# Half of a projection down, moved from the second scan stage to the second ranking stage of a one-core kernel

## The reference, cut to what matters

```python
x = x + tanh(g_xattn) * mamba(ctx_1024, gate=layernorm(x))     # 4 batches, 1024 steps, 1024 channels, 16 states
h = layernorm(x)
scores = h @ w_router;  idx = sort(top_k(scores, 128))         # 128 rows of each batch
sel = h[b, idx]                                                # 4 x 128 rows
x1  = sel + attention(rms_norm(sel)) @ wo                      # causal over the 512 rows
h2  = rms_norm(x1)
mlp = (silu(h2 @ w_gate) * (h2 @ w_up)) @ w_down               # w_down: 4096 x 1024
out[b, idx] = sigmoid(score) * (x1 + mlp) + (1 - sigmoid(score)) * sel
x = x + tanh(g_ffn) * out
```

## Time and profile before

| what | us |
|---|---|
| median of 3 runs | 3016.49 |
| lowest and highest | 3014.51, 3021.93 |
| the profiled execution's own time | 3018.8 |
| its span, first to last instruction | 3017.1 |

### The profile page before, as it was taken

How to read it: one execution, slowest core, us unless ns; L and a number is a source line. 1 busy time by engine, 2 the same in 40 slices (tenths; PEclk the granted TensorE clock), 3 DMA queues, 4 the chain that set the end, 5 groups by cost and what they waited for, 6 DMA issues and landing times. The chain is left out here.

```text
span 3017.1 us, 30047 instructions
## 1 busy us (share of the span) xinstructions
PE 2392.6 (79%) x10552; PEld 1599.2 (53%) x10552; DVE 2110.9 (70%) x2626; ACT 1338.0 (44%) x2470; POOL 1683.2 (56%) x600
## 2 busy tenths in 40 slices
PE   7857777778777547986888888888883299999998
PEld 3334444444444326653767666654552186668863
DVE  4569999999999674432999999999997633310000
ACT  3457755566655342242665555665552212410000
POOL 1169999999999401003998898999993100000000
PEclk9969999989999758998999999999997599999999
DMA  7722252342522396745236335336333543144543
GB/s 259 253 90 75 67 158 77 113 139 63 164 66 60 115 374 208 287 134 189 84 105 197 99 104 186 109 98 216 98 108 133 204 170 98 50 144 151 152 153 104
DMA packets 224869, 426.70 MB, mean 141 GB/s; under 512 B 17488, under 2 KB 101712, under 8 KB 221904
## 3 DMA queue, kind: packets, MB, share of 16 engines
q1 hardware_dynamic: 211216, 368.68, 38.3%
q10 hardware_dynamic: 12160, 51.39, 4.3%
q0 software_dynamic: 1344, 4.72, 0.4%
HBM read 340.84 MB, written 83.89 MB: 141 GB/s over the span
## 5 line engine op out<-in xcount | busy, mean ns | idle before, releaser
L600 POOL TENSOR_TENSOR s_x<-s_du,k_bB 128x2048 f32<-128x2048 f32 x256 | 1156.3, 4533 | 80.8 <-PE s_py L663 52.0
L896 ACT ACTIVATE s_pA<-s_delta,k_negA 128x512 f32<-128x512 f32 x1024 | 664.1, 680 | 382.7 <-DVE s_x L947 373.9
L663 PE MATMUL s_py<-k_ident,s_x 128*128 128x128 f32 x4096 | 582.8, 289 | 260.6 <-DVE s_x L947 253.2
L663 PEld LDWEIGHTS s_py<-k_ident,s_x 128*128 128x128 f32 x4096 | 506.8, 150 | 489.3 <-DVE s_x L947 347.2
L962 DVE TENSOR_TENSOR_SCAN s_pA<-s_pA,s_x 128x512 f32<-128x512 f32 x384 | 452.2, 1214 | 40.9 <-POOL s_x L600 38.3
L947 DVE TENSOR_TENSOR s_x<-s_pA,k_bC 128x1024 f32<-128x1024 f32 x384 | 464.2, 1209 | 19.1 <-DMA k_bC<-scratch_xd 19.0
L962 DVE TENSOR_TENSOR_SCAN s_pA<-s_pA,s_carry,s_x 128x512 f32<-128x512 f32 x384 | 472.6, 1275 | 2.0 <-POOL s_x L600 1.6
L1570 PE MATMUL l_p<-l_hT,l_ring 128*128 128x256 f32 x1792 | 397.0, 381 | 2.5 <-DVE l_hT L1784 1.4
L1570 PEld LDWEIGHTS l_p<-l_hT,l_ring 128*128 128x128 f32 x1792 | 341.9, 191 | 50.2 <-issue 2.0
L607 POOL TENSOR_TENSOR s_x<-s_hp,k_bC 128x1024 f32<-128x1024 f32 x128 | 302.2, 2361 | 15.8 <-DVE s_hp L962 15.5
L1577 PE MATMUL l_p<-l_ring,l_hidden 128*128 128x512 f32 x512 | 220.9, 592 | 1.7 <-DMA l_ring<-in_wo 1.7
(11 more groups left out here) (200 smaller groups left out, 3100.1 us busy)
## 6 DMA issues: line engine op xcount, KB each, us to landing
k_bB<-scratch_xd SPq DMA_DIRECT2D x32, 1024.0 KB, 11.8
k_bC<-scratch_xd SPq DMA_DIRECT2D x32, 1024.0 KB, 12.3
scratch_ug<-p_ug ACTq DMA_DIRECT2D x16, 1024.0 KB, 4.0
k_u<-scratch_ug SPq DMA_DIRECT2D x64, 256.0 KB, 3.6
s_gy<-scratch_ug SPq DMA_DIRECT2D x64, 256.0 KB, 4.2
s_xt<-in_x SPq DMA_DIRECT2D x64, 256.0 KB, 4.6
scratch_x<-s_xt SPq DMA_DIRECT2D x64, 256.0 KB, 3.2
r_x<-scratch_x SPq DMA_DIRECT2D x32, 512.0 KB, 11.4
```

Of the source, the lines that this page charges most:

```text
L600: pool.tensor_tensor(out=x[:, 4 * g:4 * g + 4], in0=du[:, s % 2:s % 2 + 1].broadcast_to([P, 4, HALF]), in1=bB[:, 4 * g:4 * g + 4], op=ALU. ...
L663: last = nc.tensor.matmul(py[:, a], x[:, n, a * P:(a + 1) * P], ident[:], is_transpose=True, start=False, stop=is_last and a == HALF // P - 1)
L896: nc.scalar.activation(pA[:, n % 4], delta[:, s % 2], ACT.Exp, scale=negA[:, s % NE, n:n + 1]).then_inc(dA_ready, 1)
```

## The change: what it does

The second half of the projection down leaves the second scan. The second ranking stage takes it over, with a weight ring, result buffer, two PSUM banks and copy of its own. PE does 32 of its 64 matmuls ahead of `spread(0)` and 32 between `spread(0)` and `spread(1)`. SP puts four of its 16 weight transfers (512 KB each) between the tiles' transfers, one behind each second tile, and the other 12 behind the last tile, each of them once PE has freed a buffer. ACT's copy stands behind its last store. `FILL` gets 21 slots for each unit in place of 25. The fill now ends with the first half, and its copy moves behind the last unit.

`hidden` becomes a buffer that lives through all stages (`Through`). To make room, other buffers of other stages are laid into it: `ctxT` of the projection, `ctxT` and `diagC` of the first scan, `u`, `xd` and `pick` of the first ranking stage. Those stages run the same instructions as before; so do both layer stages.

```diff
-FILL = (2, 2, 3, 3, 3, 3, 4, 5)
+FILL = (2, 2, 2, 3, 3, 3, 3, 3)
-TILES_UP, TILES_ALL = 2 * NI, 3 * NI
+TILES_UP, TILES_ALL = 2 * NI, 2 * NI + NI // 2
-DOWN_FROM = (GATE_UP + 10, GATE_UP + 16 + DOWN_HALF)
-FILL_END = DOWN_FROM[1] + DOWN_HALF
+DOWN_FROM = GATE_UP + 10
+FILL_END = DOWN_FROM + DOWN_HALF
...
@@ scan_stage
-            def down(h, m, a):
-                tile = TILES_UP + (h * NI + m) // 2
+            def down(m, a):
+                tile = TILES_UP + m // 2
...
-                if q == fill_slot(DOWN_FROM[0] + DOWN_HALF - 1) + COPY_LAG and i == 1:
-                    copy_down(0)
...
@@ route_stage, sync
+            def load_weights(j):
+                if j >= RING:
+                    sp.wait_ge(w_used, j - RING + 1)
+                sp.dma_start(ring[:, j % RING].rearrange("p (a c) -> p a c", c=HALF),
+                             t["w_down"][2 * j * P:(2 * j + 2) * P, HALF:].rearrange("(a p) c -> p a c", p=P)).then_inc(w_in[j % RING], 16)
+
+            if not late:
+                sp.dma_start(coef[:], t["coef0"]).then_inc(coef_in, 16)
             for k in range(2, SPAN * TILES):
                 load(k)
+                if not late and k % 2 and k // 2 <= RING:
+                    load_weights(k // 2 - 1)
...
+            if not late:
+                for j in range(RING, NI // 2):
+                    load_weights(j)
+                sp.wait_ge(down_copied, SPAN)
+                sp.dma_start(t["mlp0"][:, HALF:].rearrange("(a p) c -> p a c", p=P), down[:]).then_inc(coef_in, 16)
...
@@ route_stage, scalar, behind the last store
+            if not late:
+                act.wait_ge(coef_in, 16)
+                act.wait_ge(w_used, NI // 2)
+                for a in range(SPAN):
+                    nc.scalar.activation(down[:, a], p_down[a][:], ACT.Copy, scale=coef[:, a:a + 1]).then_inc(down_copied, 1)
...
@@ route_stage, tensor
+            def feed_forward(begin, end):
+                for m in range(begin, end):
+                    if m % 2 == 0:
+                        pe.wait_ge(w_in[m // 2 % RING], 16 * (m // 2 // RING) + 16)
+                    for a in range(SPAN):
+                        last = nc.tensor.matmul(p_down[a][:], keep.hidden[:, m, a * P:(a + 1) * P],
+                                                ring[:, m // 2 % RING, m % 2 * HALF:(m % 2 + 1) * HALF], start=m == 0, stop=m == NI - 1)
+                    if m % 2:
+                        last.then_inc(w_used, 1)
...
+            else:
+                feed_forward(0, NI // 2)
             spread(0)
...
+            else:
+                feed_forward(NI // 2, NI)
             spread(1)
```

More of the change, by code:

```diff
@@ L59, in halves, with __init__ @@
     return ap[:, h * HALF:(h + 1) * HALF]
+class Through:
+    def __init__(self, nc, ctx):
+        self.hidden = ctx.enter_context(nc.sbuf_tensor("t_hidden", [P, NI, ROWS], F32))
 class Kept:
-    def __init__(self, nc, ctx):
+    def __init__(self, nc, ctx, through):
+        self.hidden = through.hidden
         def sb(name, shape):
@@ L360, in scan_stage @@
         h2T = sb("h2T", [P, KT, ROWS])
[L361 removed]
+        hidden = keep.hidden
         ring = sb("ring", [P, RING, KT * P])
@@ L372, in scan_stage @@
         swish_ready, hidden_ready = sem("swish_ready"), sem("hidden_ready")
-        down_copied, down_out = sem("down_copied"), [sem(f"down_out{j}") for j in range(2)]
+        down_copied, down_out = sem("down_copied"), sem("down_out")
     if early:
         w_in = sb("w_in", [P, 2, NK, P])
-        ctxT = sb("ctxT", [P, 2, NK, HALF])
+        space = keep.hidden[:].rearrange("p m r -> p (m r)")
+        ctxT = space[:, 0:2 * NK * HALF].rearrange("p (j k l) -> p j k l", j=2, k=NK)
         conv = sb("conv", [P, NE, TAPS + 1])
-        diagC = sb("diagC", [P, NE, TAPS, P])
+        diagC = space[:, 2 * NK * HALF:].rearrange("p (e i c) -> p e i c", e=NE, i=TAPS)
         raw = sb("raw", [P, 2, TAPS - 1 + HALF])
@@ L512, in load_weights @@
                 else:
-                    h, j = (k - TILES_UP) // (NI // 2), (k - TILES_UP) % (NI // 2)
-                    src = t["w_down"][2 * j * P:(2 * j + 2) * P, h * HALF:(h + 1) * HALF].rearrange("(a p) c -> p a c", p=P)
+                    j = k - TILES_UP
+                    src = t["w_down"][2 * j * P:(2 * j + 2) * P, 0:HALF].rearrange("(a p) c -> p a c", p=P)
                     sp.dma_start(ring[:, k % RING].rearrange("p (a c) -> p a c", c=HALF), src).then_inc(w_in[k % RING], 16)
[L517 to L520, removed]
             load_end(0)
@@ L565, in _ @@
                         load_weights(k)
-                if fill and s == UNITS - 3:
-                    store_down(0)
             store(UNITS - 1)
@@ L682, in gate_up @@
                     last.then_inc(w_used, 1)
-            def down(h, m, a):
-                tile = TILES_UP + (h * NI + m) // 2
+            def down(m, a):
+                tile = TILES_UP + m // 2
                 if m % 2 == 0 and a == 0:
                     pe.wait_ge(w_in[tile % RING], 16 * (tile // RING) + 16)
-                if h == 0 and m == 0:
+                if m == 0:
                     pe.wait_ge(swish_ready, NI // 2)
                     pe.wait_ge(hidden_ready, NI // 2 if a else 1)
-                if h and m == 0:
-                    pe.wait_ge(down_copied, a + 1)
                 last = nc.tensor.matmul((p_gate, p_up)[a][:], hidden[:, m, a * P:(a + 1) * P],
@@ L701, in feed_forward @@
                         gate_up(k)
[L702 to L705, removed]
+                    at = k - DOWN_FROM
+                    if 0 <= at < DOWN_HALF and at % 2 == 0:
+                        down(at // (2 * SPAN), at // 2 % SPAN)
             def late_projection(s, i):
@@ L834, in gate_sigmoid, with copy_down @@
                 nc.scalar.activation(sigmoid[:], sigmoid[:], ACT.Exp).then_inc(sig_ready, 1)
[L836 to L841, removed]
+            def copy_down():
+                act.wait_ge(coef_in, 16)
+                act.wait_ge(log_ready, NI // 2)
+                act.wait_ge(swish_ready, NI // 2)
+                act.wait_ge(w_used, TILES_ALL)
                 for a in range(SPAN):
-                    if h:
-                        act.wait_ge(down_out[a], 16 * h)
                     nc.scalar.activation((size, sigmoid)[a][:], (p_gate, p_up)[a][:], ACT.Copy,
@@ L927, in _ @@
             if fill:
-                copy_down(1)
+                copy_down()
         @block.vector
@@ L1052, in route_stage @@
     late = first == 0
+    if not late:
+        ring = sb("ring", [P, RING, 2 * HALF])
+        down = sb("down", [P, SPAN, HALF])
+        pick = sb("pick", [P, TILES, P])
+        coef = sb("coef", [P, SPAN])
+        p_down = [ctx.enter_context(nc.psum_tensor(f"r_pdown{a}", [P, HALF], F32)) for a in range(SPAN)]
+        w_in, w_used, coef_in, down_copied = [sem(f"w_in{j}") for j in range(RING)], sem("w_used"), sem("coef_in"), sem("down_copied")
     if late:
-        u = sb("u", [P, LATE_BUFS, L])
+        space = keep.hidden[:].rearrange("p m r -> p (m r)")
+        u = space[:, 0:LATE_BUFS * L].rearrange("p (j l) -> p j l", l=L)
+        pick = space[:, (LATE_BUFS + 1) * L:(LATE_BUFS + 2) * L].rearrange("p (a c) -> p a c", c=P)
         w_x = sb("w_x", [P, NE, ND])
-        xd = sb("xd", [H2 * ND, SPAN, HALF])
+        xd = space[:, LATE_BUFS * L:LATE_BUFS * L + SPAN * HALF].rearrange("p (b l) -> p b l", b=SPAN)
         p_xd = [ctx.enter_context(nc.psum_tensor(f"r_pxd{b}", [H2 * ND, HALF], F32)) for b in range(SPAN)]
@@ L1105, in _ @@
             sp.wait_ge(small, 64)
+            if not late:
+                sp.wait_ge(coef_in, 32)
             if late:
@@ L1366, in layer_stage @@
     hT = sb("hT", [P, KT, ROWS])
-    hidden = sb("hidden", [P, NI, ROWS])
+    hidden = keep.hidden
     q, o = hidden[:, 0:NH], hidden[:, NH:2 * NH]
@@ L1918, in run @@
                 stage(nc, t, ctx, keep, *which)
-    with ExitStack() as outer:
-        run(STAGES, Kept(nc, outer))
-    run(LAST_STAGES, None)
+    with ExitStack() as whole:
+        through = Through(nc, whole)
+        with ExitStack() as outer:
+            run(STAGES, Kept(nc, outer, through))
+        run(LAST_STAGES, through)
 def kernel(x, ctx_1024, g_xattn, g_ffn, L0_xattn_in_proj_w, L0_xattn_conv_w, L0_xattn_conv_b, L0_xattn_x_proj_w,
```

13 lines of the change are left out of this document (6 added, 7 removed).

## The result

| | median us | lowest, highest | runs |
|---|---|---|---|
| before | 3015.02 | 3007.09, 3026.35 | 10 |
| after | 3028.53 | 3019.75, 3032.69 | 10 |

The ratio of after to before is 1.0042, with a 95% interval of 1.0029 to 1.0055: slower, by 13.5 us as medians and by 12.7 by the ratio. The forecast was 13.1 us slower. The profiled execution of after took 3030.91 us with a span of 3029.2, so its span is 12.1 us longer than that of before.

What follows compares the result with a forecast made beforehand. DVE was taken to bound the second scan, with PE room in the second ranking stage. A scan gain of 2 us and a ranking cost of 15.1 summed to +13.1 on the median 3016.49: 3029.6 us, range 3020 to 3036.

Steps and rivals of the forecast that it cites:

- The kind of cost: Second ranking stage: PE's spreads come late behind the moved matmuls, the second by 15.1 us, delaying the stage's end.
- the layout costs 0: Buffers laid into one another across stages: costed at 0, since no engine gets a new wait.
- First weight tile: Second ranking stage: 2.83 MB left at 357 GB/s take 7.9 us, so it lands at 2317.9 and PE starts.
- Fifth weight tile: Second ranking stage: queued behind the last tile of x, it lands at 2338.6.
- The pause: Second ranking stage: PE has nothing to do from 2334.2 until the fifth weight tile at 2338.6, 4.4 us.
- The restart of the clock: Second ranking stage: slow clock after PE's pause costs between 0 and 2.6 us; the middle, 1.3, was taken.
- rival B: PE stays at 1.2 GHz in the second ranking stage; second spread 63.6 us later, total 3078 us; chance 0.04.
- The second group and the end: Second ranking stage: PE's next 32 matmuls take 27.5 us without pause, DVE waits again, the result's store fits in.
- The scan: Second scan: losing 64 matmuls and 16 weight transfers can only remove stalls; gain of 2 us, bounds 0 and 12.0.
- Rival A: The second scan gives back much more, up to 12.0 us, deciding from 6.1 on; total 3019.6 us; chance 0.15.
- The total: Whole program: 13.1 us slower, 3029.6 us on the median.
- What would show it: Profile signs: second scan 0 to 4 us shorter, PE wait 3 to 6, two DVE waits about 9, stage about 107.

Runs made afterwards that it cites:

- kept warm: Changed kernel with useless matmuls on PE, six ahead of the first weight tile and four ahead of the fifth; 3030.97 us, one run.
- thick fill: Changed kernel with the FILL of the kernel before, 25 slots a unit in place of 21; 3038.14 us, one run.
- the one with both remedies: Changed kernel with eight weight buffers and a finer PE order in the second ranking stage; 3012.66 us, ratio 0.9985 to before.
- all of it: Changed kernel with eight weight buffers and finer PE orders in both ranking stages; 3005.49 us, ratio 0.9969 to before.
- the first ranking stage's run: Kernel before with only PE's order in the first ranking stage changed, spreads placed earlier among the x_dbl steps; 3012.68 us, ratio 0.9989.
- half left out: Changed kernel without the moved half: its 64 matmuls, 16 weight transfers and copy left out; 3015.41 us, ratio 0.9991 to before.
- after again: Changed kernel unaltered, profiled once more on the same chip as three other runs; 3035.12 us, one run.

## Why the prediction was right

- **The kind of cost.** Forecast: PE's spreads come late, and the delay runs on to the end of the stage. Shown: when PE's order was changed the DVE waits for spreads went away (of 11.9 us nothing is left, of 8.0 there is 1.3), and with buffers too the stage was back at 83.4. That the layout costs 0 holds within the interval of its run (1.0006, up to 1.0018).
- **First weight tile.** "It lands at 2317.9", 10.2 us into the stage. PE started after 12.6. The step that was wrong took the time for the bytes ahead of it, at the rate, as the time of landing. The rate was nearly right: the ten us that answer to 2310 to 2320 (2304.5 to 2314.5 in after) have 346 GB/s for 357. But when PE started, 12.6 us at 315 GB/s = 3.97 MB had moved, 0.76 more than the forecast's 3.21. Why is open: later tiles may have moved part of their bytes by then, or a landing may be told some time after the last byte (a transfer of 1 KB in this stage takes 1.4 us from issue to landing). No run tells the two apart. The late start itself cost nothing, for the pause behind it absorbs it (kept warm).
- **Fifth weight tile.** Forecast at 2338.6, 30.9 into the stage; it came at 33.1, by the same error: 33.1 us at 375 GB/s are 12.4 MB, and 11.6 lie ahead of it with its own. **This is 2.2 us of what the stage cost more.** The pause was 4.05 (forecast 4.4).
- **The restart of the clock.** "I take the middle, 1.3". It was 2.7, in the second profile of after 2.0 (15.70 - 13.7), and with the thick fill 2.3 (16.00). The rows showed the upper bound; I had no reason for the middle. This is up to 1.4 more. The Trainium skill ("TensorE: Matmul & The Clock Gate", section "HAM oscillation — how this bites in real kernels") says that a wait for the next slice can throw the engine back to the low clock; the trace agrees for the one pause of 4 us. It did not come at each tile: the 32 matmuls behind the first spread took 27.63 us, full clock throughout, so rival B fell.
- **The second group and the end.** 27.63 for 27.5, a store that fits, a second DVE wait of 8.0 for about 9: as forecast. In sum the second spread came 18.3 us later in place of 15.1.
- **The scan.** -2 was forecast, and this term was probably too small. The timed kernel with half of the projection left out shows -2.7, between -5.7 and 0. The other timed kernels, each less what its ranking stage differs, give more: the changed kernel 12.7 - 18.0 = -5.3, the one with both remedies -4.6 + 0.6 = -4.0, and "all of it" against the first ranking stage's run -7.2 + 1.8 + 0.2 = -5.2. The profiles' means differ by 3.0. So an estimate from these numbers is a gain of 3 to 5 us. Rival A, 6.1 and more, lies outside the interval of the half left out, and above all four values, but not outside every interval. Where in the scan the gain comes from is open: the spread of the profiles hides it.
- **The total.** Measured by medians +13.5; by the ratio +12.7, from 8.7 to 16.6. The forecast's +13.1 fits better than its parts do: the stage was 3 us too low (18.0 for 15.1), and the scan's gain was too low by one to three. The two errors stand against each other. So the mechanism was right, and that the sum came out within half a us is luck.
- **"What would show it".** Scan 0 to 4 shorter: 3.3 (but see above). PE's wait 3 to 6: 4.05. DVE's wait about 9: 11.9, more, by the two terms above. The second about 9: 8.0 (2.4 of that place's wait was there before). The stage 15 us longer (107 for 92): 18.1 in this pair.

## What to carry to other kernels

Work moved onto an idle engine is not free if it stands, on an in-order queue, ahead of a small step that another engine waits for: read when that step is wanted, and put no more ahead of it than is done by then. Here the same 55 us of PE work cost 18 us in one order and nothing in another, with buffers enough that its loads come in a row. And before a wait is removed, look for the next one: in the first ranking stage the spread's order gave 5 of 13.6 us, for stores ended the stage.

## What the runs showed of the hardware

- A tile queued among others landed later than its bytes and those ahead of it would take at the rate: after 12.6 us where that reckoning gave 10.2, and after 33.1 where it gave 30.9. Why is open.
- Pauses of PE of 4.05, 4.50 and 5.09 us (after, after again, thick fill) each dropped its clock from 2.4 to 1.2 GHz, and the 16 matmuls behind them took 2.7, 2.0 and 2.3 us more than at full clock. In after again the granted clock still read 1.00 when PE took up work at 2340.2, and fell only at 2341. A pause of 1.75 us (kept warm) dropped nothing: granted clock 1.00 throughout, and 14.00 us for the 16 matmuls.
- In the first scan, the DVE scans that start from a carried value took 1318 ns on the mean in one profile of after (1276 before), and 1278 in the next profile of the same kernel. Why is open. That scan stage was no longer for it (849.6 us against 852.5).
- Three executions of the kernel before on one chip took 3010.23, 3016.54 and 3026.43 us. Of the 10 us between the last two, 8.2 are in the second scan; the listed waits of DVE there add up to 41.0 us against 36.4, so they hold about half of it. The rest stays open.
